# Top-1 experts of a fused two-layer kernel: the choice is multiplied into the transposed rows, and all experts add up in one PSUM bank

## The chip, the cores and the metric

One NeuronCore of one Trainium2 chip runs the whole program. The metric is the time of the device in microseconds (us). In the names of the profile, PE is the matmul engine and PEld its weight loads, DVE the vector engine, ACT the scalar engine, POOL GpSimd and SP the queue that issues the DMAs.

## The reference

A batch of four rows (B = 4) of 512 tokens with 128 values each goes through two layers, each an attention-like mixer and an expert stage, each followed by a residual sum and a layer norm. The change is in the last stage, the top-1 experts with a capacity:

```python
logits = xt @ wg                                   # (2048, 8)
probs = softmax(logits); idx = argmax(probs)
mask = one_hot(idx, 8)
locations = cumsum(mask, axis=0) - mask            # over all 2048 tokens
mask = mask * (locations < C)                      # C = 2048 // 8
gate = sum(probs * mask, axis=-1)
...
exp_out = einsum('ech,efh->ecf', exp_in, W) + b[:, None, :]
out = einsum('tec,ecf->tf', combine, exp_out)
```

For a token this is gate x (W[e] x + b[e]) with its expert e, and 0 where the expert is full. The kernel computes that without moving tokens.

## The kernel before

The kernel has five programs, one for each engine (`sync`, `tensor`, `scalar`, `gpsimd`, `vector`), with semaphores between them (`signal`). A batch row b has two halves: `attention(b)`, which is the first mixer in four tiles of 128 queries (`tiles`, 14 phases each, then `merges`, 3 phases), and `rest(b)`, which is the routed experts, the state-space scan and the top-1 experts. `weave` takes one phase of `attention(b)` and one phase of `rest(b - 1)` in turn, the same on each engine; the last row's `rest(3)` runs alone. A `yield` ends a phase, and phases without a statement keep the engines in step. So each engine's order is fixed when the program is built, and an engine does one instruction after the other: what stands behind a waiting instruction waits too. The last phases of `rest(b - 1)`, those of the top-1 experts, fall beside the end of tile 3 of row b. Where another row follows (b = 1 and 2), `keys(b + 1)`, the projections of the next row's keys, is woven in there as well (`both`); beside row 3 there is none.

At the end of a tile the attention does this: `pick` gathers keys by one-hot matmuls (L716), ACT copies them (L1079), DVE turns them (L1513, L1515), PE makes the picked scores (L748), DVE takes their maximum away (L1536, L1538), ACT takes the exponential, PE spreads the probabilities (L760) and makes the output (L767), ACT copies it (L1095), and SP sends it through DRAM (16 small DMAs L480, then one back, L484). With that back, DVE merges it with the local part: `merge_a` (L1368 to L1371), `merge_b` (L1379 to L1392), and PE and DVE finish the attention row (L543, L558, L1581). `keys` on PE is the transposes of X (L543), then the projections L574 to L582.

The top-1 stage of a row (512 tokens in NT = 4 groups of 128; XR holds the rows, XRT them transposed):

- PE makes the logits (L891). DVE and ACT make the probabilities, the choice `mk` and its bf16 copy (L1765 to L1792).
- PE computes for each group all eight experts at once, `top1_out(i)`: two float32 matmuls (L897), XRT of the group as the loaded weights against 512 columns of `ew` each, in two PSUM banks (`TOP1_BANKS`).
- PE counts the slots in an expert (L905 to L908); DVE makes `gate` [128, 4, 8] (L1795 to L1801), which is zero but for a kept token's own expert, and the running counts (L1804 to L1808).
- PE turns the gates (L543), ACT copies them (L1232), PE multiplies them with the biases (L920).
- DVE adds that to XR (L1813), and then for each group and each expert once Y2 = bank x gate + Y2, on 128 columns, each waiting for the one before:

```python
for e in range(4):
    done = e_used if e == 3 else vec2
    STT(out=Y2[:, i, :], in0=bank[...][:, e * P:(e + 1) * P], scalar=gate[:, i, 4 * k + e:...],
        in1=Y2[:, i, :], op0=ALU.mult, op1=ALU.add).then_inc(done.sem, done.up())
```

- `norm_sums` (L1561, L1566), `norm_scale` on ACT (L1111, L1113) and `norm_rows` (L1573) end the row; SP stores it (L522).

In rows of the profile Y2 is `Y`, the turned gates `GTs` are `XD`, `OUT` is `CV`, and each float32 matmul is counted as two instructions.

## Time and profile before

| | |
|---|---|
| three runs | 1400.54, 1401.64, 1412.11 us; median 1401.64 us |
| the profiled execution | 1411.83 us, its span 1410.0 us |
| busy PE / DVE / ACT / POOL | 905.6 / 972.0 / 594.3 / 84.2 us |
| granted TensorE clock, mean | 0.776 |

The span is the time from the first to the last instruction. No engine is busy all the time: DVE has 69% and PE 64% of the span, and which of the two holds the end changes from stage to stage. The top-1 stage comes four times, at about 522 to 561 us (row 0, beside the attention of row 1), 840 to 880 us (row 1, beside row 2), 1161 to 1199 us (row 2, beside row 3) and 1379 to 1407 us (row 3, alone).

### The profile page before, as it was taken

To read this page: it belongs to the slowest core of one execution; us is meant where nothing else is said; L and a number is where in the kernel's file an instruction comes from. 1 tells how busy PE (TensorE), PEld (TensorE's weight loads), DVE (VectorE), ACT (ScalarE), POOL (GpSimd) and SP (SyncE) were. 2 spreads that over 40 slices of the span, in tenths; PEclk is the share of its full clock that TensorE was granted. 3 is DMA by queue.
4 is the path that set the end of the run, shared out by engine and by line. 5 is a ranking of instruction groups with operands and counts; after the bars stand their busy time and mean duration, and the time that the engine had idled before them with its cause. 6 is when DMAs were issued, how large, how long until landed. Compare 5 with 4: busy or idle time off the path is not lost.

```text
span 1410.0 us, 29222 instructions
## 1 busy us (share of the span) xinstructions
PE 905.6 (64%) x11808; PEld 545.3 (39%) x11808; DVE 972.0 (69%) x2254; ACT 594.3 (42%) x1299; POOL 84.2 (6%) x56
## 2 busy tenths in 40 slices
PE   4655656777567577788566677777657566472554
PEld 2444535444334244445234244444334244240122
DVE  5345543655689987656699987655689987335985
ACT  3333332466633332476633332466643331445320
POOL 0000000011000000020000000011000000030630
PEclk8556858599758889697768889698658789676897
DMA  4110110311223210311223210211223310302420
GB/s 143 31 40 10 33 39 10 66 35 39 67 68 87 69 31 18 67 36 37 67 68 87 69 31 12 57 42 39 66 63 86 76 31 10 68 1 62 112 67 8
DMA packets 84822, 72.19 MB, mean 51 GB/s; under 512 B 24528, under 2 KB 63440, under 8 KB 84496
## 3 DMA queue, kind: packets, MB, share of 16 engines
q1 hardware_dynamic: 84688, 70.34, 19.7%
q8 instruction: 93, 1.52, 0.5%
q14 instruction: 41, 0.34, 0.1%
HBM read 66.51 MB, written 3.80 MB: 50 GB/s over the span
## 4 chain that ended last, share of the span: by engine, by line
DVE 33%; PE 20%; ACT 12%; issue 11%; DMA 3%; SPq 2%; DVEq 0%; POOL 0%; ACTq 0%; POOLq 0%
DVE SG L1727 5%; PE bank L716 3%; PE bank L543 2%; DVE Y L1820 2%; DVE XP L1740 2%; PE bank L874 2%; DVE CV L1740 2%; SPq L480 2%; ACT QBD L1063 2%; DVE bank L1727 1%; PE bank L748 1%; PE bank L824 1%; ACT relu_s L1027 1%; DVE big L1715 1%; DVE big L1702 1%
## 5 line engine op out<-in xcount | busy, mean ns | idle before, releaser
L716 PE MATMUL bank<-onehot,tparts 128*32 128x256 bf16 x3840 | 134.8, 300 | 45.3 <-DVE onehot L1506 41.6
L716 PEld LDWEIGHTS bank<-onehot,tparts 128*32 128x32 bf16 x3840 | 108.7, 105 | 80.3 <-issue 70.7
L874 PE MATMUL bank<-XP,CO 128*128 128x512 f32 x128 | 86.1, 809 | 60.6 <-DVE XP L1738 33.2
L1727 DVE TENSOR_TENSOR_SCAN SG<-big 128x512 f32<-128x512 f32 x96 | 111.7, 1205 | 0.9
L1215 ACT ACTIVATE big<-DEL,Aneg 128x512 f32<-128x512 f32 x96 | 63.8, 715 | 102.5 <-DVE SG L1727 96.7
L1027 ACT ACTIVATE relu_s<-bank,nml 128x192 f32<-128x192 f32 (+1 forms) x128 | 52.9, 426 | 112.0 <-DVE nml L1472 112.0
L874 PE MATMUL bank<-CV,CO 128*128 128x512 f32 x128 | 77.3, 735 | 32.4 <-DVE CV L1740 20.4
L1467 DVE TENSOR_REDUCE ml<-bank 128x2 f32<-128x384 f32 (+1 forms) x64 | 33.8, 569 | 71.1 <-PE bank L651 38.5
L1506 DVE TENSOR_SCALAR onehot<-ib,CO 128x1024 bf16<-128x1024 f16 x160 | 69.5, 477 | 15.7 <-PE bank L716 14.5
L748 PE MATMUL bank<-GT,QBD 128*32 128x32 f32 x3072 | 56.6, 208 | 34.9 <-DVE G L1515 22.1
L543 PE MATMUL bank<-CO,relu_s 128*128 128x128 f32 (+2 forms) x256 | 45.8, 339 | 44.7 <-ACT relu_s L1027 44.7
L748 PEld LDWEIGHTS bank<-GT,QBD 128*32 128x32 f32 x3072 | 54.4, 119 | 41.9 <-issue 41.9
L1079 ACT ACTIVATE GT<-bank 128x256 f32<-128x256 f32 x64 | 24.4, 382 | 109.4 <-PE bank L716 109.1
L874 PEld LDWEIGHTS bank<-XP,CO 128*128 128x128 f32 x128 | 28.7, 247 | 101.1 <-issue 50.4
L1513 DVE TENSOR_TENSOR GT<-bank,rank_turn 128x512 f32<-128x512 f32 x64 | 44.0, 688 | 28.5 <-ACT GT L1079 28.3
L543 PEld LDWEIGHTS bank<-CO,relu_s 128*128 128x128 f32 (+2 forms) x256 | 36.4, 162 | 56.8 <-issue 55.2
L1715 DVE TENSOR_TENSOR big<-DU,BC 128x1024 f32<-128x1024 f32 x48 | 57.7, 1201 | 0.1
L543 PE MATMUL bank<-CO,QAB 128*128 128x128 f32 x96 | 21.6, 377 | 56.2 <-DVE QAB L1410 29.5
L1063 ACT ACTIVATE QBD<-QT 32x768 f32<-32x768 f32 x64 | 53.6, 838 | 6.5 <-DVE QT L1496 5.9
L874 PEld LDWEIGHTS bank<-CV,CO 128*128 128x128 f32 x128 | 25.5, 220 | 74.1 <-DVE CV L1740 31.5
L1291 POOL TENSOR_TENSOR U<-U,big 128x512 f32<-128x512 f32 x20 | 27.5, 1375 | 435.0 <-DMA big<-comb_rows 349.1
L824 PE MATMUL bank<-XRT,W 128*128 128x512 f32 (+1 forms) x72 | 50.9, 794 | 3.6 <-DVE U L1653 3.3
(306 smaller groups left out, 2002.7 us busy)
## 6 DMA issues: line engine op xcount, KB each, us to landing
BC<-bc_rows SPq DMA_DIRECT2D x128, 256.0 KB, 4.4
ib<-idx_rows SPq DMA_DIRECT2D x64, 256.0 KB, 4.1
big<-comb_rows SPq DMA_DIRECT2D x8, 1024.0 KB, 10.0
rows_bounce<-RO SPq DMA_DIRECT2D x256, 8.5 KB
W<-w SPq DMA_DIRECT2D x1, 2818.0 KB, 14.8
RB<-rows_bounce SPq DMA_DIRECT2D x16, 136.0 KB, 2.1
X<-x SPq DMA_DIRECT2D x4, 256.0 KB, 3.0
out<-CV SPq DMA_DIRECT2D x4, 256.0 KB, 2.3
```

The costliest lines, as they stand in the source:

```text
L543: return pe.transpose(o, i_, ident[0:k, 0:k])
L716: m = mm(bank[2 + c % 2][32 * bb:32 * bb + 32, 256 * kind:256 * kind + 256], tparts[:, kt, part, 32 * kind:32 * kind + 32], onehot[:, n % ...
L748: m = mm(bank[0][32 * a:32 * a + 32, 32 * xx:32 * xx + 32], QBD[:, kind, t, :, :].rearrange("p b h -> p (b h)"), GT[:, kind, t, :], start= ...
L824: mm(bank[k0][0:rows, :], wg, XRT[:, :], start=True, stop=True).then_inc(ga_ps.sem, ga_ps.up())
L874: mm(bank[5 + j][:, :], ident, hC[(n - 1) % 2][:, j, :], start=(n == 1), stop=(n == DS)).then_inc(ysum.sem, ysum.up())
L1027: m = A(PL[:, hh, c0:224], sc, ACT.Exp, scale=SCALE, bias=nml[:, h:h + 1], accum_out=ll[:, h:h + 1])
L1063: m = A(QBD[32 * bb:32 * bb + 32, :, :, bb, :], QT[32 * bb:32 * bb + 32, :, :, :], ACT.Copy)
L1215: A(decay, DEL[:, j, :], ACT.Exp, scale=Aneg[:, j, n:n + 1]).then_inc(dA_ok.sem, dA_ok.up())
L1506: TS(onehot[:, n % 4, :], ib[:, c, :], co("pos")[:, kt:kt + 1], None, ALU.is_equal).then_inc(oh_ok.sem, oh_ok.up())
L1715: TT(dBu[:, n % 2, :, :], DU[:, :, :], BC[:, n % ROWS_AHEAD, 0:1, :].to_broadcast([P, 2, L]), ALU.mult).then_inc(dBu_ok.sem, dBu_ok.up())
L1727: m = dve.tensor_tensor_scan(state, decay, dBu[:, n % 2, j, :], 0.0, ALU.mult, ALU.add)
L1740: m = TT(hC[n % 2][:, :, :], hs[:, :, :], BC[:, n % ROWS_AHEAD, 1:2, :].to_broadcast([P, 2, L]), ALU.mult)
```

## The change

The choice is applied before the matmul instead of the gate behind it. For each expert k, PE spreads the choice of the 512 tokens over all 128 partitions, by four bf16 matmuls of `mk_bf` (one column repeated 128 times) with the identity, in bank 5 or 6 (`spread`). DVE multiplies that into XRT on 128 x 512 (`chosen`), into one of four buffers `XG` (which are U and DU). PE multiplies the result with the 128 columns of that expert, four groups, in float32, and adds to what stands in bank 7 (`product`). The biases, now with the turned choice instead of the turned gate (turned in bank 6), are the last that is added to bank 7. Then DVE takes four `STT`: Y2 = bank 7 x gate + XR, with `ps1`, the sum of a token's gates over the experts. The first `top1_out`, which stood two phases earlier on PE, has nothing in its place.

```diff
--- before.py
+++ after.py
@@ -227,6 +227,7 @@
+        XG = (U[:, 0, :], U[:, 1, :], DU[:, 0, :], DU[:, 1, :])
         YG = CV
 
         pr = sb("pr", [P, 4, NT, NE2])
@@ -379,9 +380,10 @@
-        bias_ps = signal("bias_in_psum", 1)
-        e_ps = signal("top1_out_in_psum", 2 * NT)
-        e_used = signal("top1_out_used", 2 * NT)
+        mb_ps = signal("choice_spread_in_psum", NE2)
+        xg_ok = signal("chosen_rows_ready", NE2)
+        xg_used = signal("chosen_rows_used", NE2)
+        e_ps = signal("top1_out_in_psum", 1)
...
@@ -892,12 +894,21 @@
                 m.then_inc(rl_ps.sem, rl_ps.up())
                 yield
 
-                def top1_out(i):
-                    for k in range(2):
-                        mm(bank[TOP1_BANKS[i][k]][:, :], XRT[:, i * P:(i + 1) * P], w("ew")[:, k * 512:(k + 1) * 512],
-                           start=True, stop=True).then_inc(e_ps.sem, e_ps.up())
-
-                top1_out(0)
+                def spread(k):
+                    if k >= 2:
+                        pe.wait_ge(xg_ok.sem, xg_ok.at(b, k - 1))
+                    for i in range(NT):
+                        m = mm(bank[5 + k % 2][:, i * P:(i + 1) * P], mk_bf[:, i, k:k + 1].to_broadcast([P, P]), ident_bf[:, :],
+                               start=True, stop=True)
+                    m.then_inc(mb_ps.sem, mb_ps.up())
+
+                def product(k):
+                    pe.wait_ge(xg_ok.sem, xg_ok.at(b, k + 1))
+                    for i in range(NT):
+                        m = mm(bank[7][:, i * P:(i + 1) * P], XG[k % 4][:, i * P:(i + 1) * P], w("ew")[:, k * P:(k + 1) * P],
+                               start=(k == 0 and i == 0), stop=False, skip_group_check=True)
+                    m.then_inc(xg_used.sem, xg_used.up())
+
                 yield
                 pe.wait_ge(mk_ok.sem, mk_ok.at(b, 1))
                 for i in range(NT):
@@ -907,29 +918,37 @@
                         mm(o, ones_bf[:, :], mk_bf[:, k, :], start=False, stop=False)
                     m = mm(o, ones_bf[:, :], cum_bf[:, :], start=False, stop=True)
                 m.then_inc(loc_ps.sem, loc_ps.up())
+                spread(0)
                 yield
                 pe.wait_ge(gate_ok.sem, gate_ok.at(b, 1))
                 pe.sem_inc(hold_pe, 1)
                 for i in range(NT):
-                    m = turn(bank[7][0:NE2, i * P:(i + 1) * P], gate[:, i, :])
+                    m = turn(bank[6][0:NE2, i * P:(i + 1) * P], mk[:, i, :])
                 m.then_inc(gT_ps.sem, gT_ps.up())
                 yield
                 pe.wait_ge(gT_sb.sem, gT_sb.at(b, 1))
-                pe.sem_inc(hold_pe, 1)
-                for i in range(NT):
-                    m = mm(bank[7][:, i * P:(i + 1) * P], GTs[:, i * P:(i + 1) * P], w("eb")[0:NE2, :], start=True, stop=True)
-                m.then_inc(bias_ps.sem, bias_ps.up())
-                yield
-                top1_out(1)
-                yield
-                pe.wait_ge(e_used.sem, e_used.at(b, 2))
-                pe.sem_inc(hold_pe, 1)
-                top1_out(2)
-                pe.wait_ge(e_used.sem, e_used.at(b, 5))
-                pe.sem_inc(hold_pe, 1)
-                top1_out(3)
-                for _ in range(4):
-                    yield
+                spread(1)
+                yield
+                for k in range(2):
+                    product(k)
+                    spread(k + 2)
+                yield
+                for k in range(2, 4):
+                    product(k)
+                    spread(k + 2)
+                yield
+                for k in range(4, 6):
+                    product(k)
+                    spread(k + 2)
+                yield
+                for k in range(6, 8):
+                    product(k)
+                for i in range(NT):
+                    m = mm(bank[7][:, i * P:(i + 1) * P], GTs[:, i * P:(i + 1) * P], w("eb")[0:NE2, :], start=False, stop=True,
+                           skip_group_check=True)
+                m.then_inc(e_ps.sem, e_ps.up())
+                yield
+                yield
 
 
             pe.wait_ge(s_const, 16)
@@ -1229,7 +1248,7 @@
...
-                A(GTs[:, :], bank[7][0:NE2, :], ACT.Copy).then_inc(gT_sb.sem, gT_sb.up())
+                A(GTs[:, :], bank[6][0:NE2, :], ACT.Copy).then_inc(gT_sb.sem, gT_sb.up())
...
@@ -1800,6 +1819,14 @@
                 dve.wait_ge(vec2.sem, vec2.now(b))
                 TT(gate[:, :, :], pr[:, 3, :, :], keep[:, :, :], ALU.mult).then_inc(gate_ok.sem, gate_ok.up())
                 dve.wait_ge(gate_ok.sem, gate_ok.now(b))
+                dve.tensor_reduce(ps1[:, 1, :], gate[:, :, :], AX.X, ALU.add).then_inc(vec2.sem, vec2.up())
+                dve.wait_ge(vec2.sem, vec2.now(b))
+
+                def chosen(k):
+                    dve.wait_ge(mb_ps.sem, mb_ps.at(b, k + 1))
+                    if k >= 4:
+                        dve.wait_ge(xg_used.sem, xg_used.at(b, k - 3))
+                    TT(XG[k % 4], XRT[:, :], bank[5 + k % 2][:, :], ALU.mult).then_inc(xg_ok.sem, xg_ok.up())
 
                 dve.tensor_reduce(csum[:, :], mk[:, :, :].rearrange("p n e -> p e n"), AX.X, ALU.add).then_inc(vec2.sem, vec2.up())
                 dve.wait_ge(vec2.sem, vec2.now(b))
@@ -1807,22 +1834,22 @@
                 dve.wait_ge(vec2.sem, vec2.now(b))
                 CP(cum_bf[:, :], cum[:, :]).then_inc(vec2.sem, vec2.up())
                 dve.wait_ge(vec2.sem, vec2.now(b))
-                yield
-                yield
-                dve.wait_ge(bias_ps.sem, bias_ps.at(b, 1))
-                TT(Y2[:, :, :], bank[7][:, :].rearrange("p (n d) -> p n d", n=NT), XR[:, :, :], ALU.add).then_inc(vec2.sem, vec2.up())
-                dve.wait_ge(vec2.sem, vec2.now(b))
-                for i in range(NT):
-                    for k in range(2):
-                        dve.wait_ge(e_ps.sem, e_ps.at(b, 2 * i + k + 1))
-                        for e in range(4):
-                            done = e_used if e == 3 else vec2
-                            STT(out=Y2[:, i, :], in0=bank[TOP1_BANKS[i][k]][:, e * P:(e + 1) * P], scalar=gate[:, i, 4 * k + e:4 * k + e + 1],
-                                in1=Y2[:, i, :], op0=ALU.mult, op1=ALU.add).then_inc(done.sem, done.up())
-                            dve.wait_ge(done.sem, done.now(b))
-                    if i == NT - 1:
-                        norm_sums(b, Y2)
-                    yield
+                chosen(0)
+                yield
+                chosen(1)
+                yield
+                for k in (2, 4, 6):
+                    chosen(k)
+                    chosen(k + 1)
+                    yield
+                dve.wait_ge(e_ps.sem, e_ps.at(b, 1))
+                for i in range(NT):
+                    m = STT(out=Y2[:, i, :], in0=bank[7][:, i * P:(i + 1) * P], scalar=ps1[:, 1, i:i + 1], in1=XR[:, i, :],
+                            op0=ALU.mult, op1=ALU.add)
+                m.then_inc(vec2.sem, vec2.up())
+                dve.wait_ge(vec2.sem, vec2.now(b))
+                norm_sums(b, Y2)
+                yield
                 norm_rows(b, Y2, 4, OUT, rest_done)
                 yield
 
@@ -1890,14 +1917,13 @@
...
-PER = {"vec": 81, "vec2": 70, "vec_k": 2, "act": 8, "act2": 37, "act_k": 2}
+PER = {"vec": 81, "vec2": 47, "vec_k": 2, "act": 8, "act2": 37, "act_k": 2}
...
-TOP1_BANKS = ((5, 6), (2, 3), (5, 6), (7, 5))
```

What stands on PE behind the picked scores of tile 3 (L748 before, L750 in the change), while row 0's top-1 stage runs beside row 1. Before (`XD` are the turned gates, `XRT` the turned rows):

```order
L748 MATMUL bank<-GT,QBD 32x32 x95
L920 MATMUL bank<-W,XD 128x128 [waits gates_t_in_sbuf]
L920 MATMUL bank<-W,XD 128x128 x3
L897 MATMUL bank<-W,XRT 128x512 x2
L760 MATMUL bank<-CO,PR 32x32 [waits picked_probs_ready]
L760 MATMUL bank<-CO,PR 32x32 x31
L767 MATMUL bank<-G,PBD 32x32 [waits picked_probs_spread]
L767 MATMUL bank<-G,PBD 32x32 x31
```

And in the change (L901 is `spread`, L908 `product`, `U` the buffers of experts 0 and 1):

```order
L901 MATMUL bank<-ident_bf,mk_bf 128x128 [waits gates_t_in_sbuf]
L901 MATMUL bank<-ident_bf,mk_bf 128x128 x3
L908 MATMUL bank<-W,U 128x128 [waits chosen_rows_ready]
L908 MATMUL bank<-W,U 128x128 x3
L901 MATMUL bank<-ident_bf,mk_bf 128x128 [waits chosen_rows_ready]
L901 MATMUL bank<-ident_bf,mk_bf 128x128 x3
L908 MATMUL bank<-W,U 128x128 [waits chosen_rows_ready]
L908 MATMUL bank<-W,U 128x128 x3
L901 MATMUL bank<-ident_bf,mk_bf 128x128 [waits chosen_rows_ready]
L901 MATMUL bank<-ident_bf,mk_bf 128x128 x3
L762 MATMUL bank<-CO,PR 32x32 [waits picked_probs_ready]
L762 MATMUL bank<-CO,PR 32x32 x31
```

Two products and three spreads stand between the scores and L762 (before L760), where the bias and one `top1_out` stood.

The same place on DVE. Before, from the turned keys to the sum of the picked probabilities:

```order
L1515 STREAM_TRANSPOSE G<-bank 128x256
L1536 TENSOR_REDUCE RO<-bank 128x8 [waits picked_out_stored,picked_scores_in_psum]
L1538 TENSOR_TENSOR SRd<-bank,RO 128x256 [waits vector_step]
L1813 TENSOR_TENSOR Y<-bank,XR 128x512 [waits bias_in_psum,picked_scores_shifted]
L1820 SCALAR_TENSOR_TENSOR Y<-bank,gate,Y 128x128 [waits top1_out_in_psum,vector_step_rest]
L1820 SCALAR_TENSOR_TENSOR Y<-bank,gate,Y 128x128 [waits vector_step_rest] x3
L1820 SCALAR_TENSOR_TENSOR Y<-bank,gate,Y 128x128 [waits top1_out_in_psum,top1_out_used]
L1820 SCALAR_TENSOR_TENSOR Y<-bank,gate,Y 128x128 [waits vector_step_rest] x3
L1545 TENSOR_REDUCE RO<-PR 128x8 [waits picked_probs_ready,top1_out_used]
```

And in the change (L1829 is `chosen`):

```order
L1829 TENSOR_TENSOR U<-XRT,bank 128x512 [waits choice_spread_in_psum,vector_step_rest]
L1532 TENSOR_TENSOR GT<-bank,rank_turn 128x2x256 [waits picked_latents_ready]
L1534 STREAM_TRANSPOSE G<-bank 128x256
L1829 TENSOR_TENSOR U<-XRT,bank 128x512 [waits choice_spread_in_psum]
L1555 TENSOR_REDUCE RO<-bank 128x8 [waits picked_out_stored,picked_scores_in_psum]
L1557 TENSOR_TENSOR SRd<-bank,RO 128x256 [waits vector_step]
L1829 TENSOR_TENSOR DU<-XRT,bank 128x512 [waits choice_spread_in_psum,picked_scores_shifted]
L1829 TENSOR_TENSOR DU<-XRT,bank 128x512 [waits choice_spread_in_psum]
L1564 TENSOR_REDUCE RO<-PR 128x8 [waits picked_probs_ready]
```

The `chosen` of expert 0 now stands ahead of the turned keys, that of expert 1 ahead of L1555 (before L1536), and the nine instructions of the bias and the first group are gone.

The end of the row on PE, with the next row's projections. Before:

```order
L897 MATMUL bank<-W,XRT 128x512 [waits top1_out_used]
L897 MATMUL bank<-W,XRT 128x512
L897 MATMUL bank<-W,XRT 128x512 [waits top1_out_used]
L897 MATMUL bank<-W,XRT 128x512
L574 MATMUL bank<-XT,W 128x512 [waits picked_latents_ready,picked_keys_ready,picked_out_in_sbuf,xt_in_sbuf]
L575 MATMUL bank<-XT,W 128x512
L576 MATMUL bank<-XT,W 128x512
L578 MATMUL bank<-XT,W 64x512 [waits proj_in_sbuf]
L580 MATMUL bank<-W,XT 128x64 x4
L582 MATMUL bank<-W,XT 64x32 x3
L543 MATMUL bank<-CO,On 128x128 [waits attn_rows_ready]
```

And in the change, behind the last of the projections (L584, before L582) and the product of expert 4 with its spread:

```order
L908 MATMUL bank<-W,U 128x128 [waits chosen_rows_ready]
L908 MATMUL bank<-W,U 128x128 x3
L901 MATMUL bank<-ident_bf,mk_bf 128x128 [waits chosen_rows_ready]
L901 MATMUL bank<-ident_bf,mk_bf 128x128 x3
L908 MATMUL bank<-W,DU 128x128 [waits chosen_rows_ready]
L908 MATMUL bank<-W,DU 128x128 x3
L908 MATMUL bank<-W,DU 128x128 [waits chosen_rows_ready]
L908 MATMUL bank<-W,DU 128x128 x3
L947 MATMUL bank<-W,XD 128x128 x4
L545 MATMUL bank<-CO,On 128x128 [waits attn_rows_ready]
```

Before, all of `top1_out` stood ahead of the projections; in the change the products of experts 2 and 3 stand ahead of them, and those of experts 4 to 7 with the biases behind them.

The same place on DVE. Before:

```order
L1820 SCALAR_TENSOR_TENSOR Y<-bank,gate,Y 128x128 [waits top1_out_in_psum,top1_out_used]
L1820 SCALAR_TENSOR_TENSOR Y<-bank,gate,Y 128x128 [waits vector_step_rest] x3
L1561 BN_STATS stats<-Y 128x6 [waits top1_out_used]
L1561 BN_STATS stats<-Y 128x6 x3
L1566 BN_AGGR mv<-stats 128x2 [waits vector_step_rest]
L1566 BN_AGGR mv<-stats 128x2 x3
L1368 TENSOR_TENSOR mj<-ml,RB 128x8 [waits picked_out_back,variances_ready]
```

And in the change:

```order
L1829 TENSOR_TENSOR U<-XRT,bank 128x512 [waits chosen_rows_used,choice_spread_in_psum] x2
L1829 TENSOR_TENSOR DU<-XRT,bank 128x512 [waits chosen_rows_used,choice_spread_in_psum] x2
L1847 SCALAR_TENSOR_TENSOR Y<-bank,ps,XR 128x128 [waits top1_out_in_psum]
L1847 SCALAR_TENSOR_TENSOR Y<-bank,ps,XR 128x128 x3
L1580 BN_STATS stats<-Y 128x6 [waits vector_step_rest]
L1580 BN_STATS stats<-Y 128x6 x3
L1585 BN_AGGR mv<-stats 128x2 [waits vector_step_rest]
L1585 BN_AGGR mv<-stats 128x2 x3
L1387 TENSOR_TENSOR mj<-ml,RB 128x8 [waits picked_out_back,variances_ready]
```

The merge of the attention (L1368, in the change L1387) stands behind the end of the top-1 stage in both; ahead of it there are now four `chosen`, and four STT that wait for the whole of bank 7 (`top1_out_in_psum`).

## Rows read from the trace of the kernel before

**Rows 1.** The page: busy time, the chain that ended last, a DMA with its landing.
```profile
PE 905.6 (64%) x11808; PEld 545.3 (39%) x11808; DVE 972.0 (69%) x2254; ACT 594.3 (42%) x1299; POOL 84.2 (6%) x56
...
DVE 33%; PE 20%; ACT 12%; issue 11%; DMA 3%; SPq 2%; DVEq 0%; POOL 0%; ACTq 0%; POOLq 0%
...
RB<-rows_bounce SPq DMA_DIRECT2D x16, 136.0 KB, 2.1
```

**Rows 2.** Groups by line and form: busy us, mean ns of one, idle before.
```profile
L1820 DVE SCALAR_TENSOR_TENSOR Y<-bank,gate,Y 128x128 f32<-128x128 f32 x128 | 44.9, 351 | 4.5
```

**Rows 3.** Timeline, row 0: start us, us, engine, line, what; picks to scores.
```profile
532.70 0.18 DVE L1792 CAST mk_bf<-mk 128x32 bf16<-128x32 f32 x1
...
533.91 2.81 PE L716 MATMUL bank<-onehot,tparts 128*32 128x256 bf16 x96
...
536.55 0.17 DVE L1808 CAST cum_bf<-cum 128x8 bf16<-128x8 f32 x1
...
537.26 0.69 DVE L1513 TENSOR_TENSOR GT<-bank,rank_turn 128x512 f32<-128x512 f32 x1 [0.54 <-ACT GT L1079]
```

**Rows 4.** Timeline, row 0, behind the scores.
```profile
541.63 0.43 DVE L1536 TENSOR_REDUCE RO<-bank 128x8 f32<-128x256 f32 x1 [3.32 <-PE bank L748]
...
542.60 1.99 PE L897 MATMUL bank<-W,XRT 128*128 128x512 f32 x4
...
544.52 0.76 PE L760 MATMUL bank<-CO,PR 128*32 128x32 f32 x64
```

**Rows 5.** Timeline, row 0, the end of the row with the next row's projections.
```profile
546.93 9.23 DVE L1820 SCALAR_TENSOR_TENSOR Y<-bank,gate,Y 128x128 f32<-128x128 f32 x24
...
551.67 1.96 PE L897 MATMUL bank<-W,XRT 128*128 128x512 f32 x4 [1.61 <-DVE Y L1820]
553.46 1.02 PE L574 MATMUL bank<-XT,W 128*128 128x512 f32 x2
...
554.95 0.35 SPq L484 DMA_DIRECT2D RB<-rows_bounce  x1
...
557.73 0.17 DVE L1368 TENSOR_TENSOR mj<-ml,RB 128x8 f32<-128x8 f32 x1
...
558.17 0.54 PE L582 MATMUL bank<-W,XT 128*64 128x32 f32 x6
...
560.33 1.11 DVE L1573 TENSOR_SCALAR CV<-Y,mv,rstd 128x128 f32<-128x128 f32 x4 [2.15 <-ACT rstd L1113]
...
561.48 0.17 DVE L1379 TENSOR_TENSOR den<-ll,em 128x8 f32<-128x8 f32 x1
```

**Rows 6.** Timeline, row 2, beside row 3, where no projections follow.
```profile
1186.81 0.75 PE L767 MATMUL bank<-G,PBD 128*32 128x32 f32 x64 [1.72 <-ACT PBD L1087]
...
1197.55 0.17 DVE L1368 TENSOR_TENSOR mj<-ml,RB 128x8 f32<-128x8 f32 x1
...
1199.34 0.17 DVE L1379 TENSOR_TENSOR den<-ll,em 128x8 f32<-128x8 f32 x1
```

**Rows 7.** Timeline, row 3, alone.
```profile
1371.40 3.41 PE L881 MATMUL bank<-W,CV 128*128 128x128 f32 x16 [2.84 <-DVE CV L1750]
...
1388.83 1.97 PE L920 MATMUL bank<-W,XD 8*128 8x128 f32 x8 [0.77 <-ACT XD L1232]
...
1391.64 12.33 DVE L1820 SCALAR_TENSOR_TENSOR Y<-bank,gate,Y 128x128 f32<-128x128 f32 x32
```

**Rows 8.** Timeline, rows 1 and 2: matmuls that are like the new ones.
```profile
1146.92 0.49 PE L640 MATMUL bank<-lmask_bf,ident_bf 128*128 128x192 bf16 x4
...
1153.38 2.05 PE L881 MATMUL bank<-W,CV 128*128 128x128 f32 x16 [0.73 <-DVE CV L1750]
```

**Rows 9.** Windows: length, PE (x), PEld (x), DVE (x), ACT (x), POOL (x), PEclk, DMA share, GB/s.
```profile
553.40:558.70 5.30, 5.30 (x23) 2.53 (x21) 4.18 (x19) 2.38 (x4) 0.00 (x0) 1.00 0.13 32
...
1388.80:1395.00 6.20, 5.84 (x13) 3.07 (x14) 3.77 (x10) 0.00 (x0) 0.00 (x0) 0.51 0.00 0
1395.00:1402.00 7.00, 4.20 (x8) 1.37 (x8) 6.36 (x19) 0.00 (x0) 0.00 (x0) 0.95 0.00 0
```

## The prediction

> **What bounds the kernel now.** I read the page first: DVE is busy 69% of the span and leads the chain that ended last with 33%, PE has 20% of it, issue 11% [rows 1]. A share says little here, since the top-1 stage comes four times beside different work. The groups by line give the target: the 128 STT of L1820 cost DVE 44.9 us with almost no idle time before them [rows 2], 11.2 us for each of the four rows. What they hold up has to be read from the timeline. There the reader is to look at the end of row 0. Behind the last STT stand `norm_sums` and `merge_a`, which starts at 557.73; the picked output that it needs was sent back at 554.95 and lands 2.1 us later, at 557.05 [rows 1, 5]. So the STT lie in the shadow of the transfer but for 0.7 us. Then comes `merge_b` at 561.48, behind `norm_rows`, which waited 2.15 us for ACT, and ACT had the key logs of the next row first; these wait for PE's projections, which end at 558.7 [rows 5]. The projections begin at 553.46 because the last `top1_out` ahead of them waited 1.61 us for DVE [rows 5]. The chain thus goes through PE's place in the queue as much as through DVE's work. Row 1 shows the same pattern.
>
> **Prices of the new work.** *Product*: eight float32 matmuls of the same form, sixteen instructions, take 2.05 us at the full clock [rows 8], less some 0.15 us of drain: 0.95 us for the four of one product. Alone and with their drain they would be 1.15; I take 0.95 in a queue that does not run dry, with 0.93 and 1.15 as bounds. At the lower clock the sixteen take 3.41 us [rows 7], 1.71 for four. *Spread*: no row shows it. The nearest are four bf16 matmuls with 192 columns, 0.49 us with their drain [rows 8]; with 128 columns I take 0.28 us, bounded by 0.1 and 0.42. The Trainium skill ("TensorE: Matmul & The Clock Gate", Back-to-back issue gap) states about 81 ns for each pair of weight load and matmul at 128 columns; by that a spread is 0.32 us, and the 28 spreads would add 1.1 us to the sum. The row with 192 columns neither proves nor excludes that. *Bias*: as a product, 0.95 (four matmuls at the lower clock took 1.97 [rows 7]). *Chosen*: DVE on 512 columns of PSUM and SBUF, 0.69 us like L1513 [rows 3]. *The last four STT*: they do not wait for each other, so less than the 0.385 us apiece that L1820 takes (9.23 / 24 [rows 5]); I take 1.1 us, bounded by 0.8 and 1.55.
>
> On PE a row then costs 8 x 0.95 + 8 x 0.28 + 0.95 = 10.8 us; before it was four `top1_out` of 1.99 [rows 4] and the bias, 9.1 us. DVE loses 11.2 + 0.7 us and gains 8 x 0.69 + 1.1 + 0.2 (the sum of the gates) = 6.8 us. So the change takes 5 us of a row from DVE, and makes it wait for PE eight times.
>
> **Rows 0 and 1, step by step** (times of row 0).
> 1. The removed first `top1_out` frees nearly 2 us of PE between picks, but the slot count behind pick 2 needs `mk_bf`, which DVE has at 532.88, and DVE works on without a gap to 536.7. Pick 3 starts at 533.91 [rows 3]; count and first spread (0.28) fit in without moving it. Gain: nothing.
> 2. On DVE the gate sum (0.22) and `chosen` 0 (0.7) now stand ahead of L1513, which had waited 0.54 us for ACT [rows 3]. Delay 0.4 us.
> 3. On PE the second spread stands behind the scores, and on DVE `chosen` 1 waits for it ahead of L1536: 0.3 + 0.1 + 0.7 = 1.1 us more, 1.5 in all for the exponential. But PE reached L760 only at 544.52, when `top1_out` was done [rows 4]. Now the scores end 0.4 later, and three spreads and two products take 2.75 us where bias and `top1_out` took 3.0: L760 starts some 0.2 us later, and all behind it, the transfer too. The wait is covered by PE's own work; without that cover it would be 1.5 us.
> 4. Before, the third `top1_out` began 551.67 - 1.61 - 1.99 = 548.1. From 548.3 on there are now two products and two spreads, 2.46 us: the projections start at 550.8 and end at 556.0, 2.6 us earlier (no wait for DVE any more).
> 5. Only then come products 4 to 7, spreads 6 and 7 and the bias: 4 x 0.95 + 2 x 0.28 + 0.95 = 5.3 us, to 561.4, with the drain 561.6. `chosen` 6 and 7 (0.7 each and some 0.2 of hand-over) fit beside the product ahead of them.
> 6. The four STT end at 562.7. From the last STT to `merge_a` it took 556.16 to 557.73, 1.57 us: `merge_a` at 564.3 instead of 557.73. In row 2, where ACT is free, `merge_b` follows 1.8 us after `merge_a` (1197.55 to 1199.34 [rows 6]): 566.1 instead of 561.48 [rows 5].
>
> `merge_b` is followed by the attention output, the norm and the next row's first tile one by one, so the delay of **4.6 us** stays; row 1 the same. What is late next is PE's bank 7, no longer the transfer or the key logs. Behind the waiting STT on DVE are queued `merge_a`, `merge_b` and the next row's key work, and for these wait PE and ACT.
>
> **Row 2** has no projections. L767 at 1186.81 [rows 6] moves to 1187.0 and ends at 1187.7; six products, four spreads and the bias are 7.8 us, to 1195.5, with drain, STT and the 1.57 us `merge_a` is at 1198.3 instead of 1197.55: **+0.8 us**.
>
> **Row 3, alone.** PE starts at 1388.8 behind the turned choice, as before. Its clock was granted 0.51 to 1395.0, the level of 1.2 GHz, and 0.95 after that [rows 9], after 6 us in which PE was busy nearly all the time. Seven spreads, eight products and the bias are 10.5 us at the full clock. With the rise where it was, 6.2 us at the lower clock do 3.5 of them, and the other 7.0 end at 1402.0; with drain and STT 1403.3, where the 32 STT ended at 1391.64 + 12.33 = 1403.97 [rows 7]: **-0.6 us**. The DVE chain of 12.3 us is replaced by a PE chain of the same length. The skill (same page, The HAM clock gate) says that the default is the throttled state and that sustained activity lifts it; by that the denser work might lift it a little earlier, up to 1 us of gain.
>
> **Sum**: 2 x 4.6 + 0.8 - 0.6 = +9.4 us on the span of 1410.0 us (1419.4; the execution took 1411.83, so 1421.2). The median of the runs lies 10 us below the profiled one, with the same program; I add the difference to it: 1401.64 + 9.4 = **1411 us**. The unknown prices: 8 products and 7 spreads a row at their low bounds take off 0.2 + 1.3 us, at the high ones add 1.6 + 1.0, in four rows -6 to +10; the STT -1 to +2. That is 1404 to 1423.
>
> **Rivals.**
> - *PE falls to the lower clock* in the densest stretch, or a spread with repeated weights is far dearer than its neighbour. Then from 1.8 times as long on: behind the projections 5.3 becomes 9.5 us, +4.2 in rows 0 and 1, some +6 in row 3 if the clock does not rise: +24 us, 1425 us. Against it: PE is at 1.00 in 553.4 to 558.7 [rows 9], and the change fills its gaps. It decides for slower by over 1% from a further 1.2 us a row on. 0.23 with the upper part of my own range.
> - *The DVE work is what counts*, and PE keeps up behind it: `merge_a` then waits for the transfer alone (0.5 us gained), the key logs come 2.6 us earlier and take the 2.15 us wait away, row 3 ends after 8 x 0.7 + 1.1 us instead of 13: 2 x 2.5 + 0.5 + 6 = 11 us faster, 1390 us. For it: the chain names L1820. Against it: the order, which puts four products behind the projections. 0.06.
> - *Nothing to measure*: products and projections slide into each other so that rows 0 and 1 lose 1 to 2 us only, for instance if PE started products 4 and 5 in the 5 us that it idles ahead of the attention output. In-order issue does let it do that; but DVE's merge waits for the same bank. +2 us, 1404 us. 0.13.
>
> The forecast keeps 0.58. By these, with a bound of 1% (14 us, about what runs of this kernel tell from nothing): slower 0.28, within 1% 0.67, faster 0.05. The range of 1402 to 1424 leaves out the fast rival and the far end of the slow one.
>
> **What the profile after would show.** L1387 (`merge_a`) of row 0 some 7 us after the landing of RB instead of 0.7; DVE idle ahead of L1847, released by PE L947 (the bias); L576 some 2.5 us earlier relative to L769; ACT's PR 1.5 us later, L762 only 0.2. I am wrong if L947 ends within 1 us of the landing, if spreads take over 0.4 us, or if DVE's `chosen` make PE wait in each step.

## The result, and the profile after

The change is slower by half a per cent: 1415.27 us (median of 20 runs) against 1409.31 us for the kernel before (20 runs), ratio 1.0048 with an interval of 1.0027 to 1.0068, which is +6.8 us (3.8 to 9.6). The profiled execution took 1419.35 us, its span is 1417.4 us, 7.4 us more than the span before.

The page of the change, its parts on busy time and on the chain that ended last:

```profile
PE 911.4 (64%) x12128; PEld 570.0 (40%) x12128; DVE 952.0 (67%) x2174; ACT 593.6 (42%) x1299; POOL 83.9 (6%) x56
...
DVE 33%; PE 21%; ACT 13%; issue 11%; DMA 2%; SPq 1%; DVEq 0%; POOL 0%; ACTq 0%; POOLq 0%
DVE SG L1746 5%; PE bank L545 3%; PE bank L908 2%; DVE XP L1759 2%; ACT QBD L1082 2%; DVE CV L1759 2%; PE bank L876 2%; PE bank L718 2%; DVE onehot L1525 1%; DVE bank L1746 1%; PE bank L826 1%; PE bank L750 1%; ACT relu_s L1046 1%; DVE big 
```

DVE lost 20 us of work against [rows 1], PE gained 6, and the time rose. L908, the new products, stand in the chain.

The new groups, by line and form (busy us, mean ns of one, idle time before and its releaser), which answer to [rows 2]:

```profile
L908 PE MATMUL bank<-W,U 128*128 128x128 f32 x128 | 19.7, 301 | 0.0
L908 PE MATMUL bank<-W,DU 128*128 128x128 f32 x128 | 17.6, 287 | 0.0
L901 PE MATMUL bank<-ident_bf,mk_bf 128*128 128x128 bf16 x128 | 13.3, 230 | 0.7 <-ACT XD L1251 0.7
...
L1829 DVE TENSOR_TENSOR U<-XRT,bank 128x512 f32<-128x512 f32 x16 | 11.0, 688 | 26.6 <-PE bank L901 26.4
...
L1847 DVE SCALAR_TENSOR_TENSOR Y<-bank,ps,XR 128x128 f32<-128x128 f32 x16 | 4.5, 344 | 9.3 <-PE bank L947 9.3
```

The last field shows the waits: ahead of L1820 DVE sat idle for 4.5 us in all [rows 2]; now it waits 44 us for spreads ahead of the `chosen`, and 9.3 us for the bias ahead of the 16 final STT. These waits are not all loss, but they show who follows whom now: DVE follows PE.

Row 0 in the timeline, for [rows 4, 5] (it starts 3.3 us later than before, from drift in earlier stages: the norm that opens it is at 525.87, before at 522.53):

```profile
525.87 1.12 DVE L1592 TENSOR_SCALAR XR<-Y,mv,rstd 128x128 f32<-128x128 f32 x4 [0.96 <-ACT rstd L1132]
...
546.22 0.42 DVE L1555 TENSOR_REDUCE RO<-bank 128x8 f32<-128x256 f32 x1
...
547.85 0.91 PE L762 MATMUL bank<-CO,PR 128*32 128x32 f32 x64
...
554.45 1.08 PE L576 MATMUL bank<-XT,W 128*128 128x512 f32 x2
...
559.22 0.54 PE L584 MATMUL bank<-W,XT 128*64 128x32 f32 x6
...
559.66 0.35 SPq L486 DMA_DIRECT2D RB<-rows_bounce  x1
559.68 1.16 PE L908 MATMUL bank<-W,U 128*128 128x128 f32 x8
...
561.10 0.69 DVE L1829 TENSOR_TENSOR DU<-XRT,bank 128x512 f32<-128x512 f32 x1 [5.76 <-PE bank L901]
...
564.10 1.15 PE L947 MATMUL bank<-W,XD 8*128 8x128 f32 x8
565.29 1.13 DVE L1847 SCALAR_TENSOR_TENSOR Y<-bank,ps,XR 128x128 f32<-128x128 f32 x4 [2.34 <-PE bank L947]
...
568.00 0.17 DVE L1387 TENSOR_TENSOR mj<-ml,RB 128x8 f32<-128x8 f32 x1
...
568.64 1.12 DVE L1592 TENSOR_SCALAR CV<-Y,mv,rstd 128x128 f32<-128x128 f32 x4 [0.20 <-ACT rstd L1132]
...
569.79 0.17 DVE L1398 TENSOR_TENSOR den<-ll,em 128x8 f32<-128x8 f32 x1
```

The first product behind the projections (L908 at 559.68) starts with the landing still to come, and bank 7 is complete only behind L947. `merge_a` (L1387) starts 6.2 us after the picked output has landed (559.66 and 2.1 us); before it was 0.7. DVE idled 5.76 us ahead of `chosen` 6's spread and 2.34 us ahead of the STT.

To take drift out, I measure each stage from the start of the norm that opens it (L1573 before, L1592 in the change) to `merge_b` (L1379, L1398), in row 3 to the start of the last norm. All times in us, differences of starts in the timelines:

| | row 0 | row 1 | row 2 | row 3 |
|---|---|---|---|---|
| before | 38.95 | 40.26 | 38.98 | 28.35 |
| the change | 43.92 | 43.26 | 37.73 | 27.88 |
| difference | +4.97 | +3.00 | -1.25 | -0.47 |
| predicted | +4.6 | +4.6 | +0.8 | -0.6 |

The four differences add up to +6.25 us, within the measured 3.8 to 9.6. Rows 0 and 3 came as worked out. Rows 1 and 2 are 1.6 and 2.0 us better than predicted, and the cause lies before most of the new work: from the norm to the first reduce of the picked scores (L1536) the kernel before takes 19.10 us in row 0, but 20.37 and 21.07 in rows 1 and 2; the change takes 20.35, 20.35 and 20.49. So the predicted delay at that place (1.5) shows in row 0 as 1.25, and in rows 1 and 2 the kernel before has lost time of another kind there, which the change does not lose. The last section comes back to it.

One trace of each kernel says little about a single us. A second trace of each (taken later, see the experiments) has these stages:

| | row 0 | row 1 | row 2 | row 3 |
|---|---|---|---|---|
| before, second trace | 40.56 | 42.40 | 40.44 | 28.36 |
| the change, second trace | 43.77 | 45.05 | 39.93 | 27.94 |
| difference | +3.21 | +2.65 | -0.51 | -0.42 |

These add up to +4.9 us. One kernel thus differs from itself by up to 2.2 us in a row. From the first reduce to `merge_b` the picture is steadier: the change takes 3.7, 3.0 and -0.7 us more in rows 0 to 2 of the first pair and 3.6, 2.3 and -0.6 in the second.

Row 3 in the timeline of the change, for [rows 7], and the windows for [rows 9] (columns as there):

```profile
1396.98 0.61 PE L901 MATMUL bank<-ident_bf,mk_bf 128*128 128x128 bf16 x4 [0.68 <-ACT XD L1251]
1397.38 2.02 PE L908 MATMUL bank<-W,U 128*128 128x128 f32 x8
...
1404.61 1.11 PE L908 MATMUL bank<-W,U 128*128 128x128 f32 x8
...
1408.98 1.15 PE L947 MATMUL bank<-W,XD 8*128 8x128 f32 x8
1410.17 1.13 DVE L1847 SCALAR_TENSOR_TENSOR Y<-bank,ps,XR 128x128 f32<-128x128 f32 x4 [2.34 <-PE bank L947]
```

```profile
559.70:565.30 5.60, 5.55 (x49) 5.19 (x48) 1.38 (x3) 0.99 (x3) 0.00 (x0) 1.00 0.09 25
1397.00:1402.40 5.40, 5.40 (x31) 5.27 (x32) 1.67 (x3) 0.00 (x0) 0.00 (x0) 0.50 0.00 0
1402.50:1410.00 7.50, 7.50 (x71) 7.25 (x70) 3.04 (x5) 0.00 (x0) 0.00 (x0) 0.99 0.01 2
```

A product takes 2.02 us with its drain at the lower clock and 1.11 at the full one; the clock rose in the third product. In rows 0 to 2 it was at 1.00 while the last products ran (559.7 to 565.3, 883.9 to 889.4 and 1188 to 1200 us), so the rival of a falling clock did not come.

### The profile page after: what moved, and what is told of

It reads as the page before. It is cut to its first block, busy times and chain, and to the rows that moved or that the text cites. A ratio compares the mean times of both kernels' runs of the same rounds, so it can differ in the third digit from the quotient of the medians.

```text
span 1417.4 us, 29754 instructions
## 1 busy us (share of the span) xinstructions
PE 911.4 (64%) x12128; PEld 570.0 (40%) x12128; DVE 952.0 (67%) x2174; ACT 593.6 (42%) x1299; POOL 83.9 (6%) x56
## 4 chain that ended last, share of the span: by engine, by line
DVE 33%; PE 21%; ACT 13%; issue 11%; DMA 2%; SPq 1%; DVEq 0%; POOL 0%; ACTq 0%; POOLq 0%
DVE SG L1746 5%; PE bank L545 3%; PE bank L908 2%; DVE XP L1759 2%; ACT QBD L1082 2%; DVE CV L1759 2%; PE bank L876 2%; PE bank L718 2%; DVE onehot L1525 1%; DVE bank L1746 1%; PE bank L826 1%; PE bank L750 1%; ACT relu_s L1046 1%; DVE big L1734 1%; DVE big L1721 1%
## 5 line engine op out<-in xcount | busy, mean ns | idle before, releaser
L876 PE MATMUL bank<-XP,CO 128*128 128x512 f32 x128 | 82.5, 778 | 61.0 <-DVE XP L1757 33.6
L750 PE MATMUL bank<-GT,QBD 128*32 128x32 f32 x3072 | 53.6, 204 | 30.0 <-DVE G L1534 23.7
L750 PEld LDWEIGHTS bank<-GT,QBD 128*32 128x32 f32 x3072 | 51.9, 115 | 36.6 <-issue 36.6
L1532 DVE TENSOR_TENSOR GT<-bank,rank_turn 128x512 f32<-128x512 f32 x64 | 43.9, 686 | 26.2 <-ACT GT L1098 26.0
```

The source lines that it names most:

```text
L750: m = mm(bank[0][32 * a:32 * a + 32, 32 * xx:32 * xx + 32], QBD[:, kind, t, :, :].rearrange("p b h -> p (b h)"), GT[:, kind, t, :], start= ...
L876: mm(bank[5 + j][:, :], ident, hC[(n - 1) % 2][:, j, :], start=(n == 1), stop=(n == DS)).then_inc(ysum.sem, ysum.up())
```

## The experiments

**PE's place in the queue.** On PE, products 4 to 7, their spreads and the bias go ahead of the projections:

```diff
-                for k in range(2, 4):
-                    product(k)
-                    spread(k + 2)
-                yield
-                for k in range(4, 6):
-                    product(k)
-                    spread(k + 2)
-                yield
-                for k in range(6, 8):
-                    product(k)
+                for k in range(2, 8):
+                    product(k)
+                    if k < 6:
+                        spread(k + 2)
```

> The change with one edit on PE alone: products 4 to 7, their spreads and the bias stand ahead of the next row's key projections, not behind them. Theory (PE's order holds the merge): in rows 0 and 1 the final STT start about 8 us after L769 instead of 14, the projections end 5.3 us later, and with them the key logs on ACT; merge_b then waits for ACT again (norm_scale behind the logs). Merge_b 2.2 us earlier than in the change, 2.8 later than before, in rows 0 and 1; rows 2 and 3 as in the change: -4.4 us against the change, ratio to before about 1.0017 (the change had 1.0048). Rival (the cost lies in PE's added work, wherever it stands, or in the DVE hand-overs): no difference to the change, 1.0048.

Measured 1.0041 (1.0023 to 1.006), so the expected 1.0017 is missed. `merge_a` came 5.2 us earlier in rows 0 and 1 than in the change (36.88 and 36.23 us behind the opening norm instead of 42.13 and 41.46), `merge_b` only 1.7 (42.19 and 41.54). The theory holds in the trace: the place in the queue moved `merge_a` by the length of the stretch, and the next one in the row, ACT, took most of it back, since `norm_rows` (L1586) now waits 3.71 us for it:

```profile
558.02 0.17 DVE L1381 TENSOR_TENSOR mj<-ml,RB 128x8 f32<-128x8 f32 x1
...
561.55 0.28 ACT L1124 ACTIVATE lnv<-mv,eps 128x4 f32<-128x4 f32 x1
...
562.18 1.11 DVE L1586 TENSOR_SCALAR CV<-Y,mv,rstd 128x128 f32<-128x128 f32 x4 [3.71 <-ACT rstd L1126]
```

The total moved less than expected (1 us, where 4.4 was written down and 3.5 is in the two stages), and the intervals of the two kernels overlap, so the time alone does not show it. Row 2, where nothing was to change, took 39.90 us in this trace instead of 37.73; the granted clock was 0.50 in two stretches of it (1157.0 to 1159.0 and 1169.5 to 1172.7 us).

**ACT's place in the queue**, on top of that: the logs of the keys move behind `norm_scale` and the merge's exponential.

```diff
+                yield
                 act.wait_ge(kv_ps.sem, kv_ps.at(b, 1))
                 kr = bank[0][:, 0:256].rearrange(...)[:, :, 32:64]
                 softplus_logs(b, act_k, kr, [kr_e[:, s, :, :] for s in range(3)], kr_sp)
                 yield
-                yield
```

> As the kernel with the products ahead of the projections, and on ACT the key logs (L978 to L982) moved one phase on, behind norm_scale and the exponential of the merge. Theory: the second thing that is late, ACT's place for norm_scale, goes too: merge_b another 1.9 us earlier in rows 0 and 1, 0.9 us later than before; -8.2 us against the change, ratio to before about 0.999. Rival (ACT's order counts for nothing, the merge is bound elsewhere): as without this edit.

Measured 1.0011 (0.9992 to 1.003): against the kernel before no loss can be told any more. `merge_b` at 39.93 and 39.55 us, another 2.3 and 2.0 us earlier. In its timeline of row 0:

```profile
554.56 1.15 PE L941 MATMUL bank<-W,XD 8*128 8x128 f32 x8
555.50 0.35 SPq L486 DMA_DIRECT2D RB<-rows_bounce  x1
...
555.75 1.13 DVE L1841 SCALAR_TENSOR_TENSOR Y<-bank,ps,XR 128x128 f32<-128x128 f32 x4 [2.33 <-PE bank L941]
...
558.46 0.17 DVE L1381 TENSOR_TENSOR mj<-ml,RB 128x8 f32<-128x8 f32 x1
...
560.01 0.28 ACT L1124 ACTIVATE lnv<-mv,eps 128x4 f32<-128x4 f32 x1
...
560.65 1.11 DVE L1586 TENSOR_SCALAR CV<-Y,mv,rstd 128x128 f32<-128x128 f32 x4 [1.74 <-ACT rstd L1126]
...
561.80 0.17 DVE L1392 TENSOR_TENSOR den<-ll,em 128x8 f32<-128x8 f32 x1
```

The STT run before the output lands, and `norm_scale` (L1124) now waits for the copies of the projections (the wait of the norm is 1.74 us), no longer for the logs. In row 0 1.0 us is left against the kernel before (39.93 against 38.95): the last of the copies that ACT has ahead of `norm_scale` starts 37.65 us behind the opening norm, when in the kernel before `norm_scale` itself had begun (37.17).

**The same edit on the kernel before**, alone:

> The kernel before with the ACT edit alone: key logs one phase later, behind norm_scale and the merge's exponential. Theory: DVE's 2.15 us wait for rstd ahead of norm_rows goes, merge_b 1.9 us earlier in rows 0 and 1: -3.8 us, ratio 0.9973. Rival (the key logs are themselves on the path to the next row's first scores): 0 or a loss, ratio 1.000.

Measured 0.9988 (0.9967 to 1.0008), not distinguishable from nothing or from the expected 0.9973. In the trace the step is plain in row 0: `merge_b` at 37.00 us instead of 38.95, and the wait ahead of `norm_rows` is 0.20 us instead of the 2.15 of [rows 5]:

```profile
550.60 0.17 DVE L1368 TENSOR_TENSOR mj<-ml,RB 128x8 f32<-128x8 f32 x1
550.60 0.30 ACT L1111 ACTIVATE lnv<-mv,eps 128x4 f32<-128x4 f32 x1
...
551.25 1.12 DVE L1573 TENSOR_SCALAR CV<-Y,mv,rstd 128x128 f32<-128x128 f32 x4 [0.20 <-ACT rstd L1113]
551.61 0.28 ACT L959 ACTIVATE q_e<-bank 128x128 f32<-128x128 f32 x1 [0.31 <-PE bank L582]
...
552.40 0.17 DVE L1379 TENSOR_TENSOR den<-ll,em 128x8 f32<-128x8 f32 x1
```

Row 1 of the same trace took 40.22 us (40.26 before). It had lost 1.0 us more ahead of the first reduce, and the clock was at 0.50 from 849.7 to 853.0 us, in the middle of the row. This run also puts the one above in its place. With the same order on ACT the change with its products early takes 39.93 us in row 0 and the kernel before 37.00, and the ratios are 1.0011 and 0.9988. So moving the two queues does not make the new work free: some 3 us of it remain in row 0, and ACT's edit hides them in the comparison with the kernel before.

**Is DVE's time worth anything there?** Four unused multiplications in rows 0 and 1:

```diff
                 def chosen(k):
+                    if b < 2 and k == 6:
+                        for t in range(4):
+                            TT(big[:, t // 2, t % 2, :], XRT[:, :], XRT[:, :], ALU.mult)
```

> The change, with four more DVE multiplications on 128 x 512 (0.69 us each, into a buffer that is free then; results unused) ahead of the chosen of expert 6 in rows 0 and 1. Theory: DVE idles 5.8 us there for PE, so 2.8 us of work more per row cost nothing: ratio to before 1.0048 as for the change. Rival (DVE's time counts there, so that the 5 us a row it was relieved of were worth something): +5.5 us, 1.0088.

Measured 1.004 (1.0017 to 1.0064); `merge_b` at 43.49 and 43.54 us, as without them. 2.8 us of DVE work a row cost nothing at this place, and the rival's 1.0088 lies outside the interval. Seen the other way, at least 2.8 of the 5 us a row that the change took from DVE bought nothing in these rows.

**Without experts 4 to 7** (four products and chosen less in each row, PE's and DVE's; the output lacks their weights):

> The change without experts 4 to 7: their spreads, choices and products are left out, so tokens of these experts get only their bias times the gate. Theory: in rows 0 and 1 the stretch of PE between the projections and the bias goes; merge_b 5.4 us earlier than in the change and 0.5 earlier than before. Row 2 gains 0.2 only, since the transfer lands then; row 3 4.7 us. -15.7 us against the change, ratio to before 0.9937. Rival (PE's work counts in full in every row): -19 us, 0.991. Rival (the products are hidden): rows 0 and 1 unchanged, -5 us, 1.0013.

Measured 0.9958 (0.9937 to 0.9979). `merge_b` came at 38.33 us in row 0 (5.6 earlier than in the change), row 3 took 23.14 us (4.7 less), row 2 37.29 (0.4 less). These three terms are as the theory has them. Row 1 is not: it took 40.27 us, only 3.0 less, because PE stood still for 1.77 us inside the picked scores, as the kernel before does (last section). The four stages add up to 13.8 us and the ratios to 12.7 us, not 15.7. Both rivals are out by the trace: rows 0 and 1 did change, and row 2 did hardly.

**Each spread twice in rows 0 and 1** (the range of the loop in `spread` doubled):

> The change, with each spread issued twice in rows 0 and 1 (the same four bf16 matmuls into the same bank). Theory: a spread is 0.23 us of PE and seven of them lie on the path, so merge_b of rows 0 and 1 comes 1.6 us later (45.5 us behind the norm of the scan stage instead of 43.9): +3.2 us, ratio to before 1.0071. Rival (spreads are hidden behind DVE's chosen): 43.9, no difference.

Measured 1.0089 (1.0057 to 1.0121). `merge_b` of row 0 at 44.85 us, 0.9 more than in the change and 1.4 more than in two other kernels with the same spreads (43.49 with the padding, 43.40 in the next run), where 1.6 was expected; L762 starts 0.7 later, three spreads of 0.23. Rows 1 and 2 took 46.25 and 41.40 us, but both lost time of another kind ahead of the first reduce (22.01 and 24.16 us instead of 20.35 and 20.49): PE stood still for 1.3 us in each, and in row 2, whose spreads were not doubled, the clock was at 0.50 in two stretches. So spreads are not hidden; that each costs its full PE time is shown for the first three.

**Row 3's clock.** Three float32 matmuls of 512 columns in row 3, whose results nobody reads:

```diff
+                def warm(n):
+                    for _ in range(n):
+                        mm(bank[0][:, :], XRT[:, 0:P], w("ew")[:, 0:512], start=True, stop=True)
+
+                if alone:
+                    warm(2)                       # where the first top1_out stood
...
                 m.then_inc(gT_ps.sem, gT_ps.up())
+                if alone:
+                    warm(1)                       # behind the turned choice
```

> The change, and in row 3 alone PE gets three float32 matmuls of 512 columns more whose results nobody reads: two behind the logits (where the first top1_out stood before), one behind the turned choice. Theory: in row 3 of the change the first two and a half products run at the clock of 1.2 GHz because PE idles for 3.5 us ahead of the choice; with PE kept busy they run at the full clock. The span from the norm of the scan stage to the last norm is 27.9 us in the change and comes to 25.1 (0.4 at the turn, 2.4 at products and spreads). Ratio to before 1.003. Rival (the clock falls all the same, as in the kernel before, whose matmuls in that place did not keep it to 1388.8): 27.5 to 27.9 us. Rival (the stretch is bound by DVE's part of the loop): 27.5.

Row 3 took 24.98 us instead of 27.88. The ratio is 1.0036 (1.0007 to 1.0064). In its timeline:

```profile
1390.87 3.76 PE L914 MATMUL bank<-W,XRT 128*128 128x512 f32 x4
...
1396.42 1.02 PE L914 MATMUL bank<-W,XRT 128*128 128x512 f32 x2
...
1397.28 0.38 PE L901 MATMUL bank<-ident_bf,mk_bf 128*128 128x128 bf16 x4
1397.50 1.11 PE L908 MATMUL bank<-W,U 128*128 128x128 f32 x8
...
1407.74 1.13 DVE L1855 SCALAR_TENSOR_TENSOR Y<-bank,ps,XR 128x128 f32<-128x128 f32 x4 [2.34 <-PE bank L955]
```

The first two unread matmuls run at the lower clock (3.76 us for four instructions), the third at the full one, and the first spread and product behind it take 0.38 and 1.11 us instead of 0.61 and 2.02. The choice (`mk_bf`) was ready when they ended, so they held nothing up. The clock was at 1.00 from 1396.4 to 1407.0 us, where in the change it was at 0.50 from 1397.0 to 1402.4. Both rivals fall by the trace; the ratio alone, whose interval overlaps that of the change, would not show it. Among the traces of kernels that leave row 3 as in the change this stage takes 27.5 to 27.9 us six times and 26.56 once (in the last run below), so the 2.9 us are more than chance.

**Both kernels' better parts together**: rows 0 to 2 as before with the logs moved, row 3 in the way of the change, without and with the unread matmuls.

> Rows 0 to 2 as the kernel before with the key logs of ACT one phase later, row 3 (alone) in the way of the change. Theory: rows 0 and 1 -1.9 us each, row 3 -0.45: ratio to before 0.997. Rival (the logs' edit gives nothing): 0.9997.

> The same with the three unread matmuls in row 3. Theory: rows 0 and 1 -1.9 us each, row 3 at 25.1 instead of 28.35 us: -7.1 us, ratio to before 0.995, faster than both kernels. Rival (the clock falls all the same): as without them, 0.997.

Measured 0.9976 (0.9946 to 1.0005) and 0.9939 (0.9909 to 0.9969). The second is the only kernel of this study with a complete output that is faster than the one before beyond its interval, by 8.6 us: `merge_b` of rows 0 and 1 at 38.18 and 38.32 us, row 3 at 25.10 instead of 28.35. Row 0 gained 0.8 us only, having lost 1.2 ahead of the first reduce, and row 2, which is as before, took 40.53 instead of 38.98; without the unread matmuls the rows were at 37.00, 38.21, 43.46 and 27.83 us, row 2 with the clock at 0.50 from 1173.6 to 1187.2 us.

**The kernels before and after once more**, for their traces:

> The kernel before once more, for its trace. In its first trace PE stood still without a releaser inside the picked scores of tile 3 for 1.0 us in row 1 and 1.6 us in row 2, and not in the change. If that belongs to the program (the place of the instructions), it comes back at the same matmuls with the same length; if it is chance, it is elsewhere or gone.

> The change once more, for its trace: merge_b of rows 0 and 1 again 43.9 and 43.3 us behind the norm of the scan stage, row 2 37.7, if these are the program's own times; and no still time of PE inside the picked scores.

The still time came back in the kernel before, at the same matmul of row 1 (after 178 of 192). The picked scores of row 1 in its first and its second trace:

```profile
855.83 2.90 PE L748 MATMUL bank<-GT,QBD 128*32 128x32 f32 x178 [1.20 <-DVE G L1515]
859.77 0.47 PE L748 MATMUL bank<-GT,QBD 128*32 128x32 f32 x14 [1.04 <-issue]
```

```profile
852.19 2.89 PE L748 MATMUL bank<-GT,QBD 128*32 128x32 f32 x178 [1.20 <-DVE G L1515]
856.26 0.47 PE L748 MATMUL bank<-GT,QBD 128*32 128x32 f32 x14 [1.18 <-issue]
```

In row 2 it was 1.60 and 1.52 us, both times after 131. In the change there was none inside the scores of rows 1 and 2 in either trace, but the second one lost 1.7 and 2.1 us elsewhere ahead of them (22.01 and 22.59 us to the first reduce); `merge_b` came at 43.77, 45.05 and 39.93 us. So the stage's own length is 43.3 to 43.9 us in rows 0 and 1 where nothing is lost, and the expectation on `merge_b` held for row 0 alone.

The kernel before lost time in the same way in its second trace, 1.6, 1.3 and 1.5 us ahead of the first reduce of rows 0 to 2 (20.71, 21.64 and 22.54 us instead of 19.10, 20.37 and 21.07). The place is the picks (L716), and the cause is the clock: the same matmuls of row 0, in the first trace and in the second (columns as in [rows 9]):

```profile
526.40:528.10 1.70, 1.70 (x72) 1.67 (x68) 1.14 (x3) 0.00 (x0) 0.00 (x0) 1.00 0.04 10
```

```profile
520.70:524.00 3.30, 3.30 (x76) 2.48 (x72) 1.17 (x3) 0.00 (x0) 0.00 (x0) 0.56 0.02 5
```

In row 1 of the change's second trace it was 0.53 from 846.7 to 850.0 us, in its first 1.00 from 854.2 to 856.0. Such drops come in both kernels and not at the same rows in each execution. They are one part of what makes single stages differ by 1 to 2 us.

**Does the still time hang on the removed matmuls?** The first `top1_out` put back in the change, unread, in rows 0 to 2:

```diff
+                if not alone:
+                    for n in range(2):
+                        mm(bank[5 + n][:, :], XRT[:, 0:P], w("ew")[:, n * 512:(n + 1) * 512], start=True, stop=True)
                 yield
```

> The change with the first top1_out put back on PE in rows 0 to 2 (the same four instructions between picks 1 and 2, results unread). In all five traces of kernels that have it PE stands still inside the picked scores of rows 1 and 2 for 0.9 to 1.2 and 1.3 to 1.6 us with no releaser; in six of seven traces of kernels without it there is no such time. Theory: the removed matmuls leave PE 1.4 us idle ahead of the slot count, and with them the still time comes back (2.5 us over rows 1 and 2; the first reduce of the picked scores 21 to 22.5 us behind the norm instead of 20.35 to 20.5), ratio to before 1.0067 instead of 1.0048. Rival (the still time hangs on where instructions lie in the program, which all other edits moved too): none in these rows, ratio 1.0048.

In the trace there is no still time in the scores of these rows: the first reduce comes at 20.35, 20.36 and 21.61 us, the last one late by the clock (0.50 from 1167.7 to 1170.2 us). By that my theory falls, and the rival stands. The count that I gave with it was not right: of the eight traces of kernels without the first `top1_out`, two have such still time, that with half the experts in row 1 and that with doubled spreads in rows 1 and 2. The ratio, 1.007 (1.0046 to 1.0093), is nearer to the theory's number, but its interval overlaps that of the change.

## Why the prediction was right, and where it was off

The prediction was +9.4 us and 1411 us. Measured were +6.8 us, with +9.4 just inside the interval of 3.8 to 9.6, and 1415.27 us. That 1411 lies only 4 us off has luck in it, since two errors took each other back in part: the median before was 1401.64 in the 3 runs that the forecast starts from and 1409.31 in 20 runs, 7.7 us more, and the difference was forecast 2.6 us too high. The mechanism was the one forecast; two sizes were off, the delay in rows 1 and 2 and that of the transfer.

- *Prices.* A product took 0.95 us (L908 from 545.42 to the next spread at 546.37) and a spread 0.23 (the step to the product behind it); 0.95 and 0.28 were taken. The four STT took 1.13 us, the gate sum 0.19 (0.22 to the next instruction), a `chosen` 0.69. Four STT and the bias are on the path in rows 0 and 1, as written.
- *Steps 1 to 3.* The first reduce 1.25 us later instead of 1.5, L762 at 21.98 us where L760 was at 21.99: the cover held in full, 0.2 was expected. The transfer was to be 0.2 us late as well; it was sent back 1.4 us later (L486 at 33.79 us, L484 at 32.42), since its 16 stores, which begin 0.1 us later, take 6.5 us from the first to the last instead of 5.3. They took 5.3 with half the experts too. Why is not known; in rows 0 and 1 nothing waits for it, `merge_a` being later still.
- *Steps 4 to 6.* Projections end 2.3 us earlier relative to the norm (2.6), and `merge_b` comes 4.97 us later (4.6). That `merge_a` is held by PE's place in the queue is shown by moving the products: it came 5.2 us earlier. That `merge_b` then hangs on ACT's place is shown by moving the logs (2.3 and 2.0 us), and that DVE's work is not what counts there by the padding, which cost nothing. The signs named at the end of the prediction came: `merge_a` 6.2 us behind the landing (7), DVE idle ahead of L1847 until L947 was done (2.34 us), L576 2.5 us earlier relative to L769 (2.5), ACT's PR 1.2 us later (1.5).
- *Rows 1 and 2* were mis-sized: +4.6 and +0.8 predicted, +3.0 and -1.25 in the first pair of traces. The prediction took row 1 to be like row 0, and row 2 from the times of the kernel before. In both that kernel had still time of PE inside the scores (1.04 and 1.60 us), of which the prediction did not ask whether it would stay. It did not. With it taken off the kernel before, the change is 4.0 and 0.4 us behind, and with the whole excess of these rows over row 0 ahead of the reduce (1.3 and 2.0 us) 4.3 and 0.7.
- *Row 2* had one more thing otherwise: the last to be ready is not bank 7 alone. The transfer lands at 35.75 us behind the norm and `merge_a` starts at 35.93, so the two paths end within 0.2 us of each other.
- *Row 3*: -0.47, predicted -0.6, with the lower clock in the first part of the stretch as in [rows 9]. What the lower clock costs there is shown by the unread matmuls, 2.9 us.
- *The Trainium skill*, "TensorE: Matmul & The Clock Gate", Back-to-back issue gap, gave 81 ns for a pair at 128 columns. The row (0.23 us for four, 58 ns each at the full clock) is nearer to what the same section gives for isolated matmuls (56 ns), so here 0.32 us a spread would have been 0.09 too much. The Trainium skill, the same page, The HAM clock gate, says that the throttled state is the default and that activity releases it. Row 3 agrees: in the change, where PE waits 3.5 us for the choice, the clock was at 0.50 from 1386 to 1402.4 us, and with the unread matmuls in that gap at 1.00 from 1396.4 on.
- *Rivals.* The falling clock did not come (1.00 in 559.7 to 565.3). The one that counts DVE's work fell with the sign of the result and with the padding. "Nothing to measure" (+2 us, below the interval) would need products during PE's idle time ahead of the attention output; there was no such overlap.

The sum of the parts comes out so: the stages of the first pair give +6.25 us; without the kernel before's own still time in rows 1 and 2 (2.6 us) they would give +8.9, near the +9.4 of the prediction. The size of the new work was thus nearly right, and what took the total down to +6.8 is, by these traces, that this still time went. That is an account from two traces of each kernel and not a separate measurement. The interval of the ratio is 6 us wide, and the stages outside, whose code is the same, differ by more than the terms that are compared: from `merge_b` of row 1 to the norm of row 2 the kernel before took 280.2 and 277.1 us, the change 274.4 and 280.5. What stays open is why the still time went.

## What to carry to other kernels

To relieve the busiest engine of work may gain nothing: ask where in each in-order queue the new work stands, and what was queued behind the old. Here four small products and the bias behind a neighbour's projections cost more than the 24 vector instructions at the end of the row (9.23 us), most of which lay in the shadow of a DMA. Look at the third engine's queue as well: moving ACT's logs behind the norm took the ratio from 1.0041 to 1.0011 where the products stood early. Give such an edit to the kernel before too, as a comparison: there it took 1.95 us off row 0 (the ratio, 0.9988, cannot be told from 1), so it does not count for the change. And when a stage is sized from one trace, ask which of its waits have no releaser: those need not be there after the edit.
